# Layer 3's experts: the tokens of six batches go to their chosen experts only, in pairs of tiles and singles

## What is computed

```
scores = sigmoid(x @ gate_W) * route_scale            # 8 experts
topk_scores, topk_idx = top_k(scores, 2)              # 2 of them for each token
topk_w = topk_scores / topk_scores.sum(-1)
gate_full = sum over k of topk_w * onehot(topk_idx)
h = gelu(x @ W1[e] + b1[e])                           # hidden size 128, every expert e
y = h @ W2[e] + b2[e]
out = sum over e of gate_full[e] * y + gelu(x @ Ws1 + bs1) @ Ws2 + bs2
x = x + tanh(g_ffn[3]) * out                          # x in here is the layer norm of the x before
```

## Time and profile before

| | us |
|---|---|
| median of 3 runs | 2098.84 (2093.68 to 2107.79) |
| the profiled execution | 2088.18, its span 2086.5 |

### The profile page before, as it was taken

The page is one execution under the profiler, slowest core; times in us unless marked ns, Lnnn a source line. Parts: engine busy times, 40 slices in busy tenths (PEclk is TensorE's granted clock), DMA queues, the critical chain, the costliest instruction groups (busy, mean ns, idle before and its releaser), DMA issues. The chain is left out here.

```text
span 2086.5 us, 28576 instructions
## 1 busy us (share of the span) xinstructions
PE 1883.4 (90%) x9758; PEld 1338.0 (64%) x9758; DVE 1142.3 (55%) x3199; ACT 735.1 (35%) x1680; POOL 224.5 (11%) x237
## 2 busy tenths in 40 slices
PE   6999697979989699999848689999889999998999
PEld 4666454656767557888737468887556666655665
DVE  4888585646776743223238563102346666677553
ACT  5666453355545221111125312221144333433221
POOL 1100301121101220000140230000211111000000
PEclk9999798999999899999969799999989999999999
DMA  7644103220001033544334457435210000001001
GB/s 220 180 158 155 40 1 99 82 62 21 18 10 51 31 112 112 171 153 166 127 116 131 165 208 283 124 110 175 65 30 26 26 26 26 16 11 31 16 0 41
DMA packets 151934, 187.38 MB, mean 90 GB/s; under 512 B 14697, under 2 KB 121971, under 8 KB 151795
## 3 DMA queue, kind: packets, MB, share of 16 engines
q1 hardware_dynamic: 143042, 164.31, 24.5%
q0 software_dynamic: 8192, 20.98, 3.2%
q10 hardware_dynamic: 560, 0.27, 0.0%
HBM read 130.73 MB, written 50.59 MB: 87 GB/s over the span
## 5 line engine op out<-in xcount | busy, mean ns | idle before, releaser
L1236 PEld LDWEIGHTS a_t<-kept_ident,a_probs 128*128 128x128 f32 x1280 | 142.3, 145 | 108.0 <-issue 66.7
L1593 DVE COPY a_probsT<-a_t 128x512 f32<-128x512 f32 x320 | 205.0, 682 | 4.5 <-PE a_t L1236 2.4
L1236 PE MATMUL a_t<-kept_ident,a_probs 128*128 128x128 f32 x1280 | 183.3, 286 | 25.4 <-DVE a_probsT L1593 24.7
L1220 PE MATMUL a_s<-a_kT,a_qT 32*128 32x256 f32 (+2 forms) x1024 | 185.5, 471 | 10.1 <-ACT a_probs L1374 5.3
L1251 PE MATMUL a_o_bank<-a_probsT,a_v 128*64 128x256 f32 (+1 forms) x1280 | 172.0, 399 | 9.1 <-ACT a_o_raw L1396 6.6
L2738 PE MATMUL r_bank<-r_w,r_hT 128*128 x624 | 139.3, 379 | 1.0 <-DVE r_hT L2882 1.0
L1368 ACT ACTIVATE a_probs<-a_s,a_negmax 128x512 f32<-128x512 f32 x128 | 86.8, 683 | 144.1 <-DVE a_negmax L1572 142.3
L1378 ACT ACTIVATE a_probs<-a_s,a_negmax 128x256 f32<-128x256 f32 x256 | 102.2, 472 | 96.9 <-DVE a_negmax L1576 96.4
L2738 PEld LDWEIGHTS r_bank<-r_w,r_hT 128*128 128x128 f32 x624 | 118.2, 190 | 23.0 <-issue 7.6
L1576 DVE CUSTOM_DVE_ANT_0 a_s<-a_s,a_mask_bias 128x256 f32<-128x256 f32 x256 | 101.1, 457 | 55.4 <-PE a_s L1220 36.5
L1220 PEld LDWEIGHTS a_s<-a_kT,a_qT 32*128 32x128 f32 (+1 forms) x1024 | 88.1, 190 | 62.7 <-issue 35.9
(11 more groups left out here) (380 smaller groups left out, 3275.8 us busy)
## 6 DMA issues: line engine op xcount, KB each, us to landing
r_firsts<-in_f_w SPq DMA_DIRECT2D x27, 1024.0 KB, 5.2
r_firsts<-in_f_w SPq DMA_DIRECT2D x46, 512.0 KB, 4.6
slots_in<-a_zeros SPq DMA_DIRECT2D x8, 2048.0 KB
half_in<-a_zeros SPq DMA_DIRECT2D x8, 1024.0 KB
r_w<-in_f_w SPq DMA_DIRECT2D x8, 1024.0 KB
r_xg<-slots_in SPq DMA_DIRECT2D x28, 256.0 KB, 3.5
slots_out<-r_y SPq DMA_DIRECT2D x28, 256.0 KB, 2.1
r_w_raw<-in_f_w SPq DMA_DIRECT2D x16, 384.0 KB
```

What stands on the lines that cost most here:

```text
L1220: last = nc.tensor.matmul(out, qT[rows, e % 2, m, c, t * P:(t + 1) * P], kT[rows, e % 2, c, :], start=True, stop=True)
L1236: last = nc.tensor.transpose(bank[:, n * P:(n + 1) * P], src, ident[:, :])
L1593: nc.vector.tensor_copy(dst, t_bank(n)[:, :].rearrange("p (k n) -> p k n", k=KT)).then_inc(t_free, 1)
```

## The change

Layer 3 gets the routed way for its first six batches (`sparse` = 6) and keeps the dense way for the last two and for the shared expert.

- The groups become 0-1, 2-3, 4-5, 6-7 (`QUARTERS`). The first three are chosen the routed way, in steps 30, 46 and 60 of the attention, counted in steps 32, 48 and 61 and scattered. `slot_tables` (six parts) runs in steps 62 (two parts), 63, 64 and 65 (two). It now also picks the first bias `b1_of` for each slot.
- At the end of the attention SyncE waits for the tables and loads W1 for the 12 pairs, each at an address read from the table (`load_first`), into the room of the attention's projections.
- The block of the experts (`mixed_layer`) first goes through 19 slots, 12 pairs of tiles and 7 singles: `turn_rows`, `rows_out`, `slot_hidden`, gelu, `slot_output`, `slot_out` (which adds b2 of the slot's expert), and a store to `slots_out` through a ring of four (`RY`). Among them VectorE makes batch 7's norm, the places and the last group's choice. GpSimd adds the shared expert's b2 to x for the first six batches.
- After that it goes through 12 dense steps: 8 experts on the last group of four tiles, then the shared expert on the 4 groups. GpSimd gathers the results of the slots, 24 gathers, when all are stored; VectorE adds those of batch b after dense step b+1 (`combine`).
- All nine W1 for the dense steps are loaded at the block's start, all W2 in the attention. The ring of layer 2's gathered results shrinks from 8 to 3.

```diff
+            self.totals_after = {k: b1 * TB for k, (b0, b1) in enumerate(cfg.choose_groups) if b1 == cfg.sparse}
+            self.sparse_tiles = slice(0, cfg.sparse * TB)
...
+        routed = cfg.routed and cfg.choose_groups[k][1] <= cfg.sparse
+        if routed and k == 0:
...
+    ASKED_SOON = route.cfg.sparse - 1 if route.cfg.sparse < BATCH else route.cfg.last - 1
     for b in range(route.cfg.last):
-        s = out_step(b) + (ASK_LAG if b < route.cfg.last - 1 or route.cfg.last == BATCH else 1)
+        s = out_step(b) + (ASK_LAG if b < ASKED_SOON else 1)
         extra[s].append(("f_ask", b, 0))
         extra[s + 1].append(("f_normed", b, 0))
         extra[s + 2].append(("f_turn", b, 0))
         extra[s + 3].append(("f_logits", b, 0))
     for k, (b0, b1) in enumerate(route.choose_groups[:-1]):
-        s = out_step(b1 - 1) + ASK_LAG + 4
-        assert b1 < route.cfg.last or route.cfg.last == BATCH
+        soon = b1 - 1 >= ASKED_SOON
+        s = out_step(b1 - 1) + (1 if soon else ASK_LAG) + 4
         extra[s].append(("f_exp", b0, k))
         extra[s + 1].append(("f_choose", b0, k))
-        if route.cfg.routed:
-            extra[s + 1 + COUNT_LAG].append(("f_count", b0, k))
+        extra[s + 1 + (1 if soon else COUNT_LAG)].append(("f_count", b0, k))
+        if b1 == route.cfg.sparse:
+            for n, parts in enumerate((2, 1, 1, 2)):
+                extra[s + 3 + n].append(("f_tables", b0, parts))
...
+                if kind == "f_tables":
+                    if k == 1:
+                        dve.wait_ge(next_weights.b1_in, 16)
+                    for _ in range(k):
+                        next(tables, None)
...
+    def load_first(self, engine, j, dst):
+        e = self.nc.sync.value_load(self.route.table[0:1, j:j + 1], min_val=0, max_val=E - 1)
+        engine.dma_start(dst, self.w1_view[bass.ds(e, 1), :, :, :].rearrange("o p k h -> p (o k) h")).then_inc(self.first_in[self.part_of[j]], 16)
...
+        engine.wait_ge(self.route.tabled, 1)
+        for j in range(self.cfg.pairs):
+            self.load_first(engine, j, self.pair_w1[:, j, :, :])
...
+    steps_of = [(e, DENSE) for e in range(E)] + [(E, g) for g in range(NG)]
...
+            def load_rows(j):
+                width, at = WIDTHS[j], tile_at[j]
+                row = nc.sync.value_load(route.rows[0:1, j:j + 1], min_val=0, max_val=E * TOK - width * P)
+                sp.dma_start(xg[:, at:at + width, :], slots_in[bass.ds(row, width * P), :].rearrange("(t p) d -> p t d", p=P)
+                             ).then_inc(xg_in[weights.part_of[j]], 16)
+
+            def store_rows(j):
+                width, at = WIDTHS[j], tile_at[j]
+                sp.wait_ge(o_out, j + 1)
+                sp.dma_start(slots_out[at * P:(at + width) * P, :].rearrange("(t p) d -> p t d", p=P),
+                             y[:, j % RY, 0:width, :]).then_inc(y_stored[j % RY], 16)
...
+            for k in range(LAST):
+                sp.wait_ge(route.scattered[k % 2], route.rows_sent(k))
+            sp.dma_start(shared_b2[:, :], w["b2"][E, :].partition_broadcast(P)).then_inc(shared_b2_in, 16)
+            for j in range(NS):
+                load_rows(j)
+                if j >= cfg.pairs:
+                    weights.load_first(sp, j, single_w1[:, j - cfg.pairs, :, :])
+            for e in range(NE):
+                sp.dma_start(w1[:, e, :, :], weights.w1_view[e]).then_inc(w1_in, 16)
+            sp.dma_start(b2[:, :], w["b2"]).then_inc(b2_in, 16)
+            for j in range(NS):
+                store_rows(j)
...
+            pool.wait_ge(placed, 1)
+            for i in range(RY):
+                pool.wait_ge(y_stored[i], 16 * ((NS - i + RY - 1) // RY))
+            for b in range(SPARSE):
+                for t in range(TB):
+                    for c in range(2):
+                        at = kept.y_slot[cfg.layer % 2][:, c, b * TB + t:b * TB + t + 1]
+                        pool.indirect_dma_start(y_got[:, b, c * TB + t, :], None, slots_out[:, :],
+                                                bass.IndirectOffsetOnAxis(ap=at, axis=0)).then_inc(gathered[b], 16)
...
+            experts = experts_of(0, 4)
+            pe.wait_ge(weights.landed, weights.total)
+            turn_rows(0)
+            for j in range(NS):
+                if j + 1 < NS:
+                    turn_rows(j + 1)
+                slot_hidden(j)
+                if len(experts) == j + 1 < NS:
+                    experts += experts_of(j + 1, min(j + 5, NS))
+                if j >= 1:
+                    slot_output(j - 1)
+                if j == 3:
+                    route.tensor_turn(pe, turn_bank[0], LATE).then_inc(turned_full, 1)
+                elif j == 5:
+                    pe.wait_ge(turned, 1)
+                    route.tensor_logits(turn_bank[1], LATE).then_inc(logits_full, 1)
+            slot_output(NS - 1)
...
+            def slot_out(j):
+                width = WIDTHS[j]
+                dve.wait_ge(o_full, j + 1)
+                if j >= RY:
+                    dve.wait_ge(y_stored[j % RY], 16 * (j // RY))
+                nc.vector.tensor_tensor(y[:, j % RY, 0:width, :], o_bank[j % 2][:, 0:width * D].rearrange("p (t d) -> p t d", t=width),
+                                        weights.b2_all[:, bass.ds(experts[j], 1), :].to_broadcast([P, width, D]), ALU.add
+                                        ).then_inc(o_out, 1)
...
+            def combine(b):
+                dve.wait_ge(gathered[b], 16 * 2 * TB)
+                dve.wait_ge(x_shifted, SPARSE)
+                for c in range(2):
+                    for t in range(TB):
+                        tile = b * TB + t
+                        last = nc.vector.scalar_tensor_tensor(out=kept.x[:, tile, :], in0=y_got[:, b, c * TB + t, :],
+                                                              scalar=kept.gates[cfg.layer % 2][:, c, tile:tile + 1],
+                                                              in1=kept.x[:, tile, :], op0=ALU.mult, op1=ALU.add)
+                    step(last)
...
+            routing = {1: lambda: route.vector_normed(dve, step, LATE), 6: logged,
+                       8: some(places), 9: some(places), 10: some(places), 11: some(places),
+                       12: some(choice), 13: some(choice), 14: some(choice), 15: some(choice), 16: some(choice), 17: scaled_gates}
+
             route.norm.ask(step, LATE, BATCH)
-            route.vector_normed(dve, step, LATE)
-            scale_gates(0, EARLY_GROUPS * GT)
-            add(0)
-            add(1)
-            dve.wait_ge(logits_full, 1)
-            route.vector_logits(dve, step, turn_bank[1], LATE)
-            route.vector_ask(dve, step, LAST)
-            choice = route.choose_parts(dve, step, LAST)
-            for n in range(2, 7):
+            rows_out(0)
+            dve.wait_ge(shared_b2_in, 16)
+            nc.vector.tensor_scalar(shared_b2[:, :], shared_b2[:, :], gate_col, None, ALU.mult).then_inc(shared_b2_scaled, 1)
+            for j in range(NS):
+                if j + 1 < NS:
+                    rows_out(j + 1)
+                if len(experts) == j + 1 < NS:
+                    experts += experts_of(j + 1, min(j + 5, NS))
+                if j >= 1:
+                    slot_out(j - 1)
+                if j in routing:
+                    routing[j]()
+                if j == 11:
+                    dve.sem_inc(placed, 1)
+            slot_out(NS - 1)
+            assert next(choice, None) is None and next(places, None) is None
+            for n in range(N):
                 add(n)
-                next(choice, None)
-            scale_gates(EARLY_GROUPS * GT, TILES)
-            dve.sem_inc(gates_ready, 1)
-            for n in range(7, N):
-                add(n)
+                if 1 <= n <= SPARSE:
+                    combine(n - 1)
...
-    3: Experts(3, "gelu", 128, False, False, True, True, True, True, 3, False, True, HALVES, 4, 7, 0, 0),
+    3: Experts(3, "gelu", 128, False, False, True, True, True, True, 3, True, True, QUARTERS, 4, 7, 0, 12, 6),
...
-                    ring, dt = (2, BF16) if n == 1 else (8, F32)
+                    ring, dt = (2, BF16) if n == 1 else (3, F32)
```

More of the change, by code:

```diff
@@ L3259, in __init__ @@
         self.cast, self.shared = False, True
-        self.w1, self.w2, self.early = [], [], 0
-    def load(self, engine, e):
-        pass
-    def place_shared(self, room):
-        self.place(room, room.shape[1] // (2 * D))
-        self.early = len(self.w1)
-    def place(self, room, count):
-        for i in range(count):
-            first, second = (room[:, (2 * i + n) * D:(2 * i + n + 1) * D] for n in range(2))
-            self.w1.append(first.rearrange("p (k h) -> p k h", k=DK))
-            self.w2.append(second)
@@ L3290, in dense_layer @@
     LATE = BATCH - 1
-    EARLY_GROUPS = cfg.choose_groups[LAST][0] // 2
+    SPARSE = cfg.sparse
+    DENSE = SPARSE * TB // GT
     STORES = TILES // TB
```

(66 more changed lines are left out.)

252 lines of the change are left out of this document (145 added, 107 removed).

## The result

The changed kernel takes 2113.31 us (median of 13 runs) where the kernel before, on the same chip, takes 2097.51 us (13 runs): ratio 1.0076, 95% interval 1.0057 to 1.0095. One of the 13 executions of the changed kernel took 2768.65 us at a granted clock of 0.642, and the ratio goes by the others. On a second chip the same two kernels stand at 0.9981 (0.9962 to 1.0001; 2024.91 against 2029.29 us). So the change is worth about nothing, and the ratio differs by 0.95% from chip to chip; the profiles show one part of that difference, and its cause stays open. The profiled execution of after ("after" is the changed kernel, "before" the kernel before) spans 2110.0 us against 2086.5.

What follows compares the result with a forecast made beforehand. The expert stage was taken as pure TensorE work at the upper clock. Attention +23, entry +1.5 and stage -23 gave +1.5 us, a 2088 us span, 2100 us against the 2098.84 median; range 2072 to 2126.

Steps and rivals of the forecast that it cites:

- Attention, +24.5 with the entry: Layer 3's attention: new small VectorE instructions add 23 us, and the expert stage is entered 1.5 us late.
- The price of 1.1 us per us of burst: Layer 3's attention: 22.6 us of VectorE bursts, less 1.6 hidden, each microsecond costing 1.1: +23 us, bounds +11 and +31.
- The entry's step: End of layer 3's attention: SyncE waits for tables, then issues 12 address-read loads taking 13.2 us; expert stage entered 1.5 us late.
- SyncE, first store at 34.4: Expert stage: SyncE issues all loads before its first result store, 34.4 us in; slot_out(4) waits until 36.7 us.
- Rival (a): Expert stage and attention: queues overlap better, stores begin at about 18 us, half the bursts hide; 2071 us, chance 0.22.
- the stand: Expert stage slots: TensorE idle some 17 us while slot_out(4) waits for the first result store to land.
- VectorE in the slots, 65: Expert stage: after 36.7 us VectorE sets the pace for 28.6 us, so the slots end at 65 us.
- Gathers: Expert stage: GpSimd's 24 gathers at 1.26 us start at 67.7 us, combines wait on them; stage takes 122 us.
- The stage before, 145: Old layer 3 expert stage: pure TensorE work at the upper clock, 145 us against 122 forecast after the change.
- Rival (b), the clock: Expert stage slots and gathers: TensorE drops to the lower clock; 2120 us, or 2137 with the last five steps; chance 0.15.
- Rival (c): Bursts at 1.4 per us (+8), dearer register reads (+4), loads 1.2 us apart (+4): 2116 us and up, chance 0.15.
- rows 4: Profile rows of mid-attention: after a choice TensorE idles 3.71 us, then seven transposes take 1.73 us, read as lower clock.

Runs made afterwards that it cites:

- the run with more bursts: Changed kernel with 24 more small dependent VectorE copies behind each of the three choices in layer 3's attention: 2036.37 us, ratio 1.0042 to the kernel before.
- the second profile: The changed kernel, nothing altered, run again on another chip: 2024.91 us, ratio 0.9981 to the kernel before.

## Why the prediction was right, point by point

The forecast was 2100 us, no change; the first chip gave 2113 us and +0.76%, the second -0.19%. The forecast's sum was +24.5 in the attention and -23 in the stage. The order of the waits came out as written; the nearly even sum owes something to errors that cancel, named below.

- **Attention, +24.5 with the entry: the sum right, by luck, its two terms not.** Measured 24.7 on the first chip, 23.9 on the second. Of that 5.5 us are the late entry, where the forecast had 1.5, and 18.4 to 19.2 us the bursts, where it had 23. The price of 1.1 us per us of burst was too dear: 19 us for the 22.6 of the forecast is 0.85 (0.81 on the second chip), and the run with more bursts gives 0.8. The entry's step failed at the tables: the forecast added 0.9 us for the last table part to the time that SyncE has. In after SyncE's loads start 3.4 us behind VectorE's copies of step 65 (1959.07 to 1962.49), but from these copies to VectorE's end and the entry that it would allow (1970.4) it is 11.4 us, little more than the 11.2 of before: the last table parts lengthen this way by next to nothing and take from SyncE's time instead of adding to it. Start, loads and entry, 3.4 + 13.0 + 0.5 us, are 5.5 us over 11.4. No run took these loads away.
- **SyncE, first store at 34.4: right** (35.3; slot_out(4) at 38.2 for 36.7). Reads in a row are 1.1 us apart. Rival (a) falls with that, and two runs show the 15 to 17 us that the stand costs.
- **VectorE in the slots, 65: 3.2 us short** (68.2). Of these, 1.5 us came in with slot_out(4); nothing in the runs parts the other 1.7.
- **Gathers: right** (first at 70.9 for 67.7, all of it the 3.2; 24 at 1.26 us). On the faster chips the combines wait 1.5 us each, the stage takes 123.6 to 124.8 us for 122. On the first chip it took 134.0: the 12 us too many go with the stretch from 2061 to 2081, which the forecast had no step for.
- **The stage before, 145: right for its execution, not for the two later ones.** The 10.7 us between that execution and its median were carried over as a constant. In the two later profiles the stage is 9 and 12 us longer, from the clock in the shared steps, three of whose four bias products the change takes out. So the median before may hold a cost that the sum against the fast execution did not see; how often the clock falls there, three profiles do not say.
- **Rival (b), the clock: half right in place, wrong in price.** It is 0.77 in the first 38 us of the stage and 0.88 in the second part, but 1.00 while gathers are waited for (1973 to 2005 of the second profile). The Trainium skill ("TensorE: Matmul & The Clock Gate", "HAM oscillation — how this bites in real kernels") tells of bursts of matmuls that are each shorter than the wait for data behind them and each start at the lower clock. The trace agrees where waits are long: the part with the stand of 17.75 us is at 0.77. It has another case in the dense steps, where TensorE is busy 28.8 of 32.0 us and the clock stays at 1.00. The forecast should not have let that sentence speak for (b): the page's case has waits longer than the bursts, the dense steps have not.
- **Rival (c): no.** The added copies made TensorE's waits longer one for one, the attention by 0.8 per us; loads were 1.1 us apart.
- **A row read short.** The forecast takes from rows 4 that seven transposes took 1.73 us; the view's window cut off the eighth, and all eight took 1.94. That this is the lower level stands all the same.

So the sum for a faster chip is +24 (attention) and -33 to -20 (stage, by which level the old shared steps ran at), and the runs put the result between, at -4 us of the median. The median of before on that chip hangs on two groups: 11 of the 23 executions of before took 2020.6 to 2023.5 us and 12 took 2029.3 to 2037.3, and the median, 2029.29, is the lowest of the upper group. Two executions more in the lower group would make the ratio 1.0007. On the first chip the slow stretch, if it is in most executions there (one was profiled), would account for some 12 of the 16 us that the median rose; what brings it is open.

## What to carry to other kernels

Before work is taken from the bound engine, write down each in-order queue that the new work passes: here 35 us of loads ahead of the first store with a ring of four results, and gathers waited for too early, cost 24 us of the stage, and bursts and loads as much again in the attention. The cures are cheap and independent: stores between loads (or a longer ring), waits three steps later, long runs of small VectorE instructions in pieces. Look too at what a queue still has to do when the other engines reach the end of a block: here the twelve loads hold the next block back by 5.5 us in every profile, and no run tried them elsewhere. And a difference under 1% between kernels that differ in indirect transfers should be timed on more than one chip.

## What the runs showed of the hardware that was not expected

- **Late signals.** In the three profiles of slow chips (the first two, and the last of before) VectorE and ScalarE wait at five to eight places, up to 19 us each, for signals that nothing in the profile explains; in the profiles of the three chips with 2029 to 2032 us no such wait is over 2.5 us, but for VectorE's 6.7 us at the entry of the changed kernel, which SyncE's loads explain. In all three profiles each place lies within a run of GpSimd's indirect transfers, 1.25 to 1.28 us apart, or within 6 us behind it. The changed kernel has 48 more of those, which would fit its worse ratio there; but the same transfers ran undisturbed elsewhere, and no run took them away on such a chip. The cause is open.
- **The clock in the old shared steps** fell to a mean of 0.60 and 0.66 in two of three profiles although TensorE is busy 33.0 of 36.9 and 29.9 of 33.8 us; in the third it was 0.96 over the same instructions. What decides is not shown.
- **GpSimd beside VectorE.** While GpSimd added the shared bias (six in 7.45 us from 1982.09), two of VectorE's normalisations took 2.54 us at 1987.14, where the same two took 0.74 us in before (1942.43). Three other profiles have 2.0 to 2.5 us there, each beside these additions; that they are the cause is argued, no run moved them. It was hidden under the stand.
